# The opening of a convolution and LoRA kernel rewritten: the gate as first factor of lora_A's mixing, turned afterwards, and zeros multiplied ahead

## The reference, cut to what matters

```python
# x (32,128,2048); y = grouped 1-d convolution of x (4 groups, 9 taps, padding 4)
y = conv(x, weight) + (cond @ c_weight.T)[:, :, None] + fside_S_0[None, :, None]
# the 32 samples x 128 channels are seen as 8 batches of rows of 2048; gate (8,16)
A_eff = einsum('bn,nri->bri', gate, lora_A)        # lora_A (16,32,2048)
B_eff = einsum('bn,nor->bor', gate, lora_B)        # lora_B (16,2048,32)
Ax    = einsum('bri,bti->btr', A_eff, y)
Ax_s  = einsum('ri,bti->btr', lora_A_shared, y)
out = x + y @ kernel + bias + einsum('bor,btr->bto', B_eff, Ax) + einsum('or,btr->bto', lora_B_shared, Ax_s)
```

## Time and profile before

| | us |
|---|---|
| median of 3 runs | 1751.65 (1750.39 to 1753.43) |
| profiled execution | 1750.7 |
| its span, first to last instruction | 1748.9 |
| TensorE busy | 1730.8 (99%) |
| VectorE busy | 983.0 (56%) |
| ScalarE busy | 666.9 (38%) |
| mean granted TensorE clock | 0.990 |

### The profile page before, as it was taken

The page is one execution under the profiler, slowest core; times in us unless marked ns, Lnnn a source line. Parts: engine busy times, 40 slices in busy tenths (PEclk is TensorE's granted clock), DMA queues, the critical chain, the costliest instruction groups (busy, mean ns, idle before and its releaser), DMA issues.

```text
span 1748.9 us, 22047 instructions
## 1 busy us (share of the span) xinstructions
PE 1730.8 (99%) x8710; PEld 1483.8 (85%) x8710; DVE 983.0 (56%) x1247; ACT 666.9 (38%) x841; POOL 35.8 (2%) x70
## 2 busy tenths in 40 slices
PE   8999999999999999999999999999999999999998
PEld 7988888888888889999999888888888888888887
DVE  7466766664444478677765544354555544464443
ACT  6465766663222277565562212132223211121110
POOL 0001100010000000000000000000000000000000
PEclk8799999999999999999999999999999999999999
DMA  8689776665765657766665676568667798887764
GB/s 233 165 254 325 275 239 233 223 231 161 238 234 196 223 199 265 272 247 242 252 251 188 220 256 210 191 201 268 223 218 235 270 336 300 303 322 261 240 239 158
DMA packets 184591, 419.61 MB, mean 240 GB/s; under 512 B 58980, under 2 KB 94660, under 8 KB 179848
## 3 DMA queue, kind: packets, MB, share of 16 engines
q1 hardware_dynamic: 174408, 381.35, 64.0%
q0 software_dynamic: 9216, 33.56, 5.1%
q10 hardware_dynamic: 864, 3.29, 0.6%
HBM read 272.11 MB, written 146.03 MB: 239 GB/s over the span
## 4 chain that ended last, share of the span: by engine, by line
PE 94%; DMA 2%; DVE 2%; ACT 1%; issue 0%; POOL 0%; SPq 0%; DVEq 0%; ACTq 0%
PE acc L1323 67%; PE cps L1226 17%; PE cps L1271 3%; PE acc L1255 3%; DMA g<-in_L_ffn_kernel 1%; PE acc L1302 1%; PE cps L1284 1%; DMA T<-g 1%; DVE x_q L891 0%; PE cps L1302 0%; PE cps L1279 0%; DMA st<-in_L_ffn_kernel 0%; DVE x_lo L898 0%; DVE g L956 0%; DVE g L952 0%
## 5 line engine op out<-in xcount | busy, mean ns | idle before, releaser
L1323 PE MATMUL acc<-w_hi,y_t 128*128 128x512 f32 x3584 | 994.3, 391 | 0.0
L1323 PEld LDWEIGHTS acc<-w_hi,y_t 128*128 128x128 f32 x3584 | 666.2, 188 | 134.9 <-issue 1.6
L1323 PE MATMUL acc<-w_lo,y_t 128*128 128x512 f32 x1792 | 553.7, 390 | 0.0
L1323 PEld LDWEIGHTS acc<-w_lo,y_t 128*128 128x128 f32 x1792 | 337.0, 188 | 71.5
L672 ACT COPY x_q<-x_raw 32x512 f32<-32x512 f32 x248 | 268.3, 1082 | 16.0 <-DVE x_lo L898 13.4
L1226 PE MATMUL cps<-cw_hi,x_hi 128*128 128x384 f32 (+2 forms) x768 | 233.3, 304 | 5.3 <-DVE x_lo L1057 2.7
L1226 PE MATMUL cps<-cw_lo,x_hi 128*128 128x384 f32 (+2 forms) x768 | 233.1, 304 | 0.0
L1226 PE MATMUL cps<-cw_hi,x_lo 128*128 128x384 f32 (+2 forms) x768 | 232.3, 302 | 0.0
L1004 DVE TENSOR_TENSOR g<-acc,g 128x1024 f32<-128x1024 f32 x96 | 117.3, 1222 | 203.1 <-PE acc L1255 115.8
L701 ACT CAST y_t<-g 128x1024 fp32r<-128x1024 f32 x96 | 101.2, 1054 | 333.2 <-PE acc L1323 302.5
L964 DVE TENSOR_TENSOR y_t<-g,y_t 128x1024 fp32r<-128x1024 f32 x96 | 117.2, 1221 | 108.8 <-ACT y_t L701 108.7
(11 more groups left out here) (101 smaller groups left out, 938.4 us busy)
## 6 DMA issues: line engine op xcount, KB each, us to landing
g<-A SPq DMA_DIRECT2D x80, 512.0 KB, 4.8
g<-U SPq DMA_DIRECT2D x80, 512.0 KB, 6.3
A<-g SPq DMA_DIRECT2D x64, 512.0 KB, 4.4
g<-in_x SPq DMA_DIRECT2D x64, 512.0 KB, 6.2
out<-g SPq DMA_DIRECT2D x64, 512.0 KB, 3.4
x_raw<-in_x SPq DMA_DIRECT2D x31, 1024.0 KB, 5.3
U<-g SPq DMA_DIRECT2D x48, 512.0 KB, 2.9
g<-in_L_ffn_kernel POOLq DMA_DIRECT2D x32, 512.0 KB, 9.1
```

Source lines behind the costliest of these rows:

```text
L1323: ins = T.matmul(acc[:, b, m, :], y_buf[b][:, c, part, :], wt[:, k % SLOTS, m * 512:(m + 1) * 512], start=(c == 0 and part == 0 and wt is ...
```

## The change

lora_A's mixing is turned round. The gate matrix, widened to 128 columns with zeros (`gate_pair`, in the buffers `ax_prev` and `ax_diff`), is now the stationary operand and lora_A the moving one: `mix_A(n)` for n = 0 to 7 takes two steps of 8 ranks at once (their sum in one bank, two products of 512 columns) for four of the 16 values of t. The moving operand reads runs of 4 elements, 16 apart. ScalarE copies each result out of `acc[:, 1]` with its columns reordered (`copy_mixed_A`), TensorE turns it in four 128 x 128 transposes into the banks of `cps` (`turn_A`), VectorE copies those to `a_stage` (`copy_turned_A`), and SP stores 4 times 512 KB instead of 8 times 256 KB. Both first steps of lora_A (2 MB) are loaded at the start, and both last ones when mixing 3 is done.

Shared lora_A is transposed between the taps of groups 1 to 3 of convolution 0. VectorE's order in convolution 0 is changed, ScalarE's x_q copies of sample 1 alternate with the splits of weight blocks 4 to 7, and VectorE's x_q copies of sample 1 come behind its split of block 7. Seven products of zeros (128 x 512, result unused) are put on TensorE: two ahead of the transposes of conv_w, three behind them, two ahead of convolution 0.

```diff
-    As_raw = g[0:RANK, 4:6, :].rearrange("p a n -> p (a n)")
+    As_raw = g[0:RANK, 0:2, :].rearrange("p a n -> p (a n)")
     gate_exp = a_raw[0:NB, 0:P]
+    zeros = g[:, 7, 0:512]
     la_raw = [g[:, 2 + 2 * b:4 + 2 * b, :].rearrange("p a n -> p (a n)") for b in range(2)]
-    a_stage = [g[:, 6 + b].rearrange("p (h b n) -> p h b n", h=2, b=NB) for b in range(2)]
+    gate_pair = [buf[:].rearrange("p (b k r) -> p b k r", b=NB, k=2) for buf in (ax_prev, ax_diff)]
+    mixed = [buf[:, i * 512:(i + 1) * 512] for buf in (b_raw, b_raw, st[:, 0], st[:, 1]) for i in range(2)]
+    a_stage = [g[:, 6 + b].rearrange("p (q n) -> p q n", q=2 * NB) for b in range(2)]
...
         def load_lora_A(k):
             if k >= 2:
-                sp.wait_ge(la_used, k - 1)
-            sp.dma_start(la_raw[k % 2], lora_A[:, k * R8:(k + 1) * R8, :]).then_inc(la_in[k % 2], 16)
+                sp.wait_ge(amix_done, 4)
+            sp.dma_start(la_raw[k % 2], lora_A[:, k * R8:(k + 1) * R8, :]).then_inc(la_in[k], 16)
...
+        def store_mixed_A(i, h):
+            sp.wait_ge(aturn_copied, 4 * i + 2 * h + 2)
+            sp.dma_start(mixed_A[h][:, :, 2 * i:2 * i + 2, :].rearrange("p b k n -> p b (k n)"),
+                         a_stage[h].rearrange("p (b k) n -> p b (k n)", b=NB)).then_inc(amix_out[h], 16)
...
         load_lora_A(0)
+        load_lora_A(1)
         sp.wait_ge(ctx_ready, 1)
         sp.dma_start(ctx_d, ctx_sum).then_inc(ctx_out, 16)
         sp.wait_ge(ctx_out, 16)
...
         load_x(1)
         for c in range(4, NCH):
             load_t(0, c)
-        sp.wait_ge(as_done, 1)
-        load_lora_A(1)
+        store_y(0)
+        load_lora_A(2)
+        load_lora_A(3)
+        sp.wait_ge(aturn_done, 4)
         load_lora_B(0)
-        store_y(0)
-        store_mixed_A(0)
-        load_lora_A(2)
+        store_mixed_A(0, 0)
+        store_mixed_A(0, 1)
         load_x(2)
         load_ctx(2)
-        store_mixed_A(1)
-        load_lora_A(3)
         store_y(1)
+        store_mixed_A(1, 0)
         load_x(3)
-        store_mixed_A(2)
-        store_mixed_A(3)
-        for b in range(2):
-            sp.wait_ge(amix_out[b], 16 * RK)
+        store_mixed_A(1, 1)
+        for h in range(2):
+            sp.wait_ge(amix_out[h], 16 * 2)
         load_a(0)
...
-                pool.wait_ge(la_used, RK)
+                pool.wait_ge(amix_done, 2 * 4)
...
+        def copy_mixed_A(n):
+            act.wait_ge(amix_done, n + 1)
+            if n == 0:
+                act.wait_ge(ctxt_done, 1)
+            elif n == 1:
+                act.wait_ge(ctx_out, 16)
+            elif n < 4:
+                act.wait_ge(aturn_done, n - 1)
+            elif n == 4:
+                act.wait_ge(w_lo_ready, NCH)
+            A.copy(mixed[n].rearrange("p (t w) -> p t w", t=4),
+                   acc[:, 1, n % 2, :].rearrange("p (w t) -> p t w", t=4)).then_inc(amix_copied, 1)
...
-        for c in range(5):
+        for c in range(4):
             split_t(0, c)
+        copy_mixed_A(0)
+        copy_mixed_A(1)
         y_hi(0)
-        for c in range(5, NCH):
-            split_t(0, c)
-        a_mixed_copy(0)
-        x_rearrange(1)
+        act.wait_ge(x_in, 16 * 2)
+        x_split_wait(act, 0)
+        x_rearrange_one(0, 0)
+        copy_mixed_A(2)
+        x_rearrange_one(0, 1)
+        copy_mixed_A(3)
+        x_rearrange_one(0, 2)
+        split_t(0, 4)
+        x_rearrange_one(0, 3)
+        split_t(0, 5)
+        x_rearrange_one(1, 0)
+        split_t(0, 6)
+        x_rearrange_one(1, 1)
+        split_t(0, 7)
+        x_rearrange_one(1, 2)
+        x_rearrange_one(1, 3).then_inc(xq_act, 1)
         x_split(1)
         perm_lora_B(0)
-        a_mixed_copy(1)
+        copy_mixed_A(4)
         x_rearrange(2)
+        copy_mixed_A(5)
         x_split(2)
         y_hi(1)
-        a_mixed_copy(2)
+        copy_mixed_A(6)
+        copy_mixed_A(7)
         copy_turn(0)
-        a_mixed_copy(3)
...
+        V.memset(zeros, 0.0).then_inc(zeros_ready, 1)
...
+        for buf in (ax_prev, ax_diff):
+            V.memset(buf[:], 0.0).then_inc(gpair_zero, 1)
...
+        def copy_turned_A(n):
+            i, j = divmod(n, 4)
+            h, c0 = j // 2, j % 2 * 4
+            dve.wait_ge(aturn_done, n + 1)
+            if i == 1 and j % 2 == 0:
+                dve.wait_ge(amix_out[h], 16)
+            V.tensor_copy(a_stage[h][:, :, c0 * R8:(c0 + 4) * R8].rearrange("p q (c r) -> p q c r", c=4),
+                          cps[:, GROUPS[j], :].rearrange("p (c q r) -> p q c r", c=4, r=R8)).then_inc(aturn_copied, 1)
...
+        split_0(1)
         rearrange_0(2, (0, 1, 2))
-        split_0(1)
+        rearrange_0(3, (0, 1))
+        split_0(2)
         dve.wait_ge(ctx_done, 1)
         V.tensor_tensor(ctx_sum, acc[0:NS, 1, 0, 0:CH], bias_bc, ALU.add).then_inc(ctx_ready, 1)
-        rearrange_0(3, (0, 1))
-        split_0(2)
         dve.wait_ge(gcol_done, 1)
         V.tensor_copy(gate_col[:], acc[:, 0, 1, 0:NB]).then_inc(gcol_ready, 1)
+        split_0(3)
         dve.wait_ge(gcol_ready, 1)
         dve.wait_ge(rep_ready, 1)
-        V.tensor_tensor(G[:], gate_col[:].unsqueeze(2).to_broadcast([P, NB, R8]),
-                        rep[:].unsqueeze(1).to_broadcast([P, NB, R8]), ALU.mult).then_inc(g_ready, 1)
-        split_0(3)
+        dve.wait_ge(gpair_zero, 2)
+        for i, dst in enumerate((G[:], gate_pair[0][:, :, 0, :], gate_pair[1][:, :, 1, :])):
+            V.tensor_tensor(dst, gate_col[:].unsqueeze(2).to_broadcast([P, NB, R8]),
+                            rep[:].unsqueeze(1).to_broadcast([P, NB, R8]), ALU.mult).then_inc(g_ready, 1)
+        for c in range(4):
+            split_t(0, c)
         dve.wait_ge(as_done, 1)
         V.tensor_copy(as_sb[:].rearrange("p h k r -> p (h k r)"), acc[:, 1, 1, :]).then_inc(as_copied, 1)
         dve.wait_ge(cb_in[0], 16)
         for i in range(GR):
-            split_t(0, i)
             y_group(0, i)
         y_lo(0)
-        for c in range(4, NCH):
-            split_t(0, c)
-        a_mixed_copy(0)
+        copy_turned_A(0)
+        copy_turned_A(1)
+        split_t(0, 4)
+        copy_turned_A(2)
+        split_t(0, 5)
+        copy_turned_A(3)
+        split_t(0, 6)
+        split_t(0, 7)
         x_rearrange(1)
         x_split(1)
         V.memset(ax_tmp[R2:P, 0:P], 0.0).then_inc(ones_zero, 1)
...
             for row in (R2, R2 + RANK):
                 ins = V.tensor_copy(ax_hl[row:row + 1, j, 1, :], ax_tmp[row:row + 1, P:2 * P])
             ins.then_inc(ones_ready, 1)
-        a_mixed_copy(1)
         x_rearrange(2)
         y_evacuate(1)
+        copy_turned_A(4)
         x_split(2)
+        copy_turned_A(5)
         y_lo(1)
-        a_mixed_copy(2)
-        a_mixed_copy(3)
+        copy_turned_A(6)
+        copy_turned_A(7)
...
-                    if v == 1 and i == 2:
-                        pe.wait_ge(amix_act, 2)
-                    if v == 1 and i == 3:
-                        pe.wait_ge(amix_dve, 2)
+                    if v in (1, 2):
+                        pe.wait_ge(aturn_copied, 4 * (v - 1) + i + 1)
...
+                    if v == 0 and 1 <= i and t < WIN:
+                        turned = T.transpose(acc[:, 1, 1, t * RANK:(t + 1) * RANK], As_raw[:, t:L:WIN],
+                                             ident[0:RANK, 0:RANK])
+                        t += 1
+                        if t == WIN:
+                            turned.then_inc(as_done, 1)
                 ins.then_inc(conv_done, 1)
...
         def mix_B(q):
             pe.wait_ge(bt_ready, q + 1)
+            if q == 0:
+                pe.wait_ge(aturn_copied, 8)
             T.matmul(cps[0:NB * R8, 1, :], G[:].rearrange("p b r -> p (b r)"), b_turn, start=True, stop=True
                      ).then_inc(bmix_done, 1)
...
+        def mix_A(n):
+            i, j = divmod(n, 4)
+            if n == 0:
+                pe.wait_ge(g_ready, 3)
                 pe.wait_ge(ctx_ready, 1)
+            if n >= 2:
+                pe.wait_ge(amix_copied, n - 1)
+            if n == 1:
                 pe.wait_ge(as_copied, 1)
...
+            for k in range(2):
+                pe.wait_ge(la_in[2 * i + k], 16)
+                ins = T.matmul(acc[:, 1, n % 2, :], (ax_prev, ax_diff)[k][:],
+                               la_raw[k].rearrange("p (w t) -> p w t", t=WIN)[:, :, 4 * j:4 * j + 4],
+                               start=(k == 0), stop=(k == 1))
+            ins.then_inc(amix_done, 1)
+        def turn_A(n):
+            i, j = divmod(n, 4)
+            pe.wait_ge(amix_copied, n + 1)
+            pe.wait_ge(y_evac, n + 1)
+            for t in range(4):
+                ins = T.transpose(cps[:, GROUPS[j], t * P:(t + 1) * P], mixed[n][:, t * P:(t + 1) * P], ident[:])
+            ins.then_inc(aturn_done, 1)
+        def keep_warm(n):
+            for _ in range(n):
+                T.matmul(acc[:, 1, 1, :], zeros[:, 0:P], zeros, start=True, stop=True)
...
+        pe.wait_ge(zeros_ready, 1)
+        keep_warm(2)
```

(64 more changed lines are left out.)

28 lines of the change are left out of this document (2 added, 26 removed).

## The result

| | before | after |
|---|---|---|
| median, us (20 runs of each) | 1750.53 (1747.31 to 1753.43) | 1753.58 (1751.4 to 1759.18) |
| profiled execution, us | 1750.7 | 1754.14 |
| its span, us | 1748.9 | 1752.3 |
| mean granted TensorE clock | 0.990 | 0.994 |

1741.5 was forecast. The ratios of the experiments are each to runs of the kernel before beside them (medians 1748.35 to 1749.72), so an experiment is compared with the change by its ratio, not by its time.

What follows compares the result with a forecast made beforehand. TensorE, busy 99% of the span, was taken to bound the kernel. The first lora sum moving from 102.52 to 92.8 saves 9.7 us: 1741.0 from the profiled 1750.7, 1741.9 from the median; 1741.5 was said, range 1734 to 1749.

Steps and rivals of the forecast that it cites:

- TensorE's own costs: Opening: convolution 0 from 12.4 to 25.1, a mixing 1.8 us, TensorE's mixing work down from 28 to 17.9 us.
- rival 1: Opening: the clock does not rise before convolution 0, which ends at 33.7, 8.6 later than forecast; total 1750; chance 0.13.
- rival 2: Mixing: moving lora_A in runs of four is slow; 3.4 us a mixing gives 1753, 5.4 gives 1767; chance 0.07.
- The mixed copy: ScalarE's copy of each mixing before its turn, reading every fourth element: bounds 0.58 and 1.09 us, taken as 1.09.
- A rule about transposes: Convolution 0: transposes do not count as a busy engine, so the clock fell behind 16 of them; turns between taps are good.
- The 16 turns of shared lora_A 1.9 as before, now between taps: Convolution 0: the turns cost 1.9 us in all between taps, and the convolution ends at 25.1 instead of 30.71.
- The first gap: Ahead of convolution 1: TensorE idles 4.6 us on x_lo; convolution 1 starts at 53.0 and takes 12.1 us, clock down.
- Such a load of 1 MB takes 7.2 us in the median; the four weight loads that GpSimd issues once the mixing is over now fall beside it, so I add 0.6: Sample 3's load, behind the store of mixed A: from 72.1 to 79.9, putting the lora sum at 92.8.
- TensorE idles 1.7 ahead of the lora sum: First lora sum: TensorE ends its third block at 91.1 and waits 1.7 us until 92.8.
- The time saved is the shift of that lora sum, 102.52, and of nothing else: First lora sum: behind it TensorE waits for next to nothing, so its shift to 92.8, 9.7 us, is the gain.
- Rival 3: Loads of lora_A's last 2 MB, sample 2 or sample 3 land 4 to 6 us later than counted: 1746; chance 0.14.
- the mild form of rival 2: Mixing at ScalarE's stride factor 1.9: 3.4 us each, 11.2 us more in all, total 1753.

Runs made afterwards that it cites:

- e3: The changed kernel without the seven products of zeros: 1757.96 us, 1.005 of the kernel before.
- e5: The changed kernel with only sample 3's load moved ahead of the last stores of mixed A, GpSimd's loads not held: 1752.15 us, 1.0018 of the kernel before.
- e9: e5 plus ScalarE's x_q copies of sample 3 ahead of its copy into the stage buffer, GpSimd not held: 1744.91 us, 0.9976 of the kernel before.
- e11: The changed kernel with the edits of e9 and e10 and the turns in one block, GpSimd not held: 1739.82 us, 0.9939 of the kernel before.
- e2: The changed kernel with GpSimd's first four loads held until sample 3 landed and sample 3's load ahead of a store of mixed A: 1743.59 us, 0.9968 of the kernel before.
- e6: The changed kernel with the 16 turns of shared lora_A in one block behind group 1 of convolution 0: 1751.14 us, 1.0018 of the kernel before.
- e7: e2 with the 16 turns in one block: 1741.88 us, 0.996 of the kernel before.
- e10: The changed kernel with VectorE's x_q copies of sample 1 ahead of its last four weight splits: 1753.25 us, 1.0018 of the kernel before.
- e4: The changed kernel with 28 unused multiplications of 128x512 put in TensorE's wait ahead of the first lora sum: 1751.07 us, 1.002 of the kernel before.
- e1: The changed kernel with GpSimd's first four 512 KB loads held until sample 3 has landed: 1751.68 us, 1.001 of the kernel before.
- e8: The kernel before with only the seven products of zeros added: 1745.22 us, 0.9984 of the kernel before.
- e12: e11 with GpSimd's first loads also held until sample 3 has landed: 1740.64 us, 0.9946 of the kernel before.

## Why the prediction was wrong

By its own steps:

- *TensorE's own costs* held but for the turns. Convolution 0 started at 12.44 (12.4 forecast) at full clock, so rival 1 falls. The start alone would not say so, as without zeros it is 12.20 (e3). A mixing took 1.8, so rival 2 falls.
- *The mixed copy* was taken at 1.09 and measured 0.59, the lower bound: 2 us too dear for four. Its nearness to the strided copies of x_q was the wrong comparison.
- *"A rule about transposes"* is not borne out as it was used: behind the same block of 16 turns the clock fell in two profiles and stayed at 1.00 in four (last section).
- *"The 16 turns of shared lora_A 1.9 as before, now between taps"* failed: 6.1. Convolution 0 ended at 29.45 and not at 25.1. That is 4.4 late; with the cheaper copies the product started 2.9 late, at 38.50 and not 35.6. The step carried over a price of a run of equal instructions to the same instructions strewn among others.
- *The first gap* was forecast at 4.6 and is 5.0, and convolution 1 at the fallen clock, 12.1, is 11.87. Its start is 56.47 instead of 53.0, late mostly by the turns.
- *"Such a load of 1 MB takes 7.2 us in the median; the four weight loads that GpSimd issues once the mixing is over now fall beside it, so I add 0.6"* failed, and decided the result. Issued at 75.49 it took 11.06. The row for the crowded case stood in the earlier trace rows, 9.4 us for lora_A. It was issued 3.4 us late (75.49 and not 72.1, nearly all of it the turns' and 0.5 SP's issue of the store ahead of it), and took 3.3 us longer than the 7.8 counted: the lora sum is 6.6 late, at 99.41 instead of 92.8. The store of mixed A beside it, 9.7 us to landing against 5.9 for the smaller ones before, was not costed at all, and by e5 ScalarE stands before it when the load is early. Taking both off the path (e9) brings the ratio from 1.0024 to 0.9976, with the turns left as they are.
- *TensorE idles 1.7 ahead of the lora sum*: 7.0, and no term stood for the clock behind it (2.6 us). The prediction priced a slow clock behind the first gap and forgot the same behind the second.
- *"The time saved is the shift of that lora sum, 102.52, and of nothing else"* failed twice. What follows hangs on the mixing of lora_B, and 3.1 at the lora sum was 0.5 there. And the stretch behind that mark was not the same: 1640.8 us against 1636.9. In e11 the mark shifts by 14.2, of which 10.6 reach the span.

Rival 3 had the mechanism, loads 4 to 6 us late, and took it alone for 1746. It came together with the turns, and by the profile the two make the draw; in the medians only the transfers' part is shown (e2, e9), the turns' part is not (e6, e7). Of the median's 3 us the profile shows none in the opening; it has 1.5 us in a wait for `b_two` and 1.5 in the clock behind the gap of 2.6 us. Whether these are systematic stays open (of the wait e5 had 0.5, e10 0.2, e4 none).

In the prediction's chances one sum is off: the forecast and rival 3 make 0.80, rival 1 and the mild form of rival 2 make 0.13 + 0.03 = 0.16, and 0.04 is left, where it gives 0.14 and 0.06.

The Trainium skill, "DMA: Bandwidth & Descriptors", Issuing engines are not separate DMA queues, says that transfers started by different engines run on the same 16 DMA engines and interleave. The trace agrees: beside GpSimd's four loads a megabyte takes 11.06 us with the DMA share at 1.03, and 7.51 where they are held back (e1).

## What to carry to other kernels

When an edit frees the main engine earlier, follow the longest chain that doesn't pass through it, transfers included, and price each transfer by a row in which the other queues are as full as they will be. Removing one of two transfers that end close together gives only the time between them, here 2.9 us of 7.2; look in the changed trace for what the waiting engine stands behind next. Take as the mark of the gain the last instruction to which later work is tied, behind any stretch where the clock has to recover, and compare the stretch behind it too.

## What the hardware showed that was not expected

- A transpose of shared lora_A (32 rows, 128 columns) costs 0.12 us in a run of 16 (1.88 in all) and 0.3 to 0.4 between the multiplications of a convolution (6.1 for 16).
- With products of zeros ahead the clock is up when convolution 0 starts: its first 384-column multiplication takes 0.69 us without them (e3) and 0.44 with them. The stretch from 25 to 30 us is at 1.00 in e3 without them too, where the earlier trace rows had 0.66.
- Behind the turns the clock falls in some executions and not in others. Strewn between taps: it fell inside convolution 0 in the profiles of e1 and e5, and not in the change, e2, e3, e4, e9 and e10, with the same turns. In a block: it fell behind the block in the kernel before and in e7 (0.66 over 20 to 25 us), and not in e6, e8, e11 and e12. A window of e1 shows a fall:

```profile
25.00:30.00 5.00, 5.00 (x21) 0.75 0.69 214
```

- ScalarE's copy of 512 columns out of PSUM with every fourth element took 0.59 us, as a plain one (0.58), while its copies of x_q, with 32 partitions, take 1.09.
